# A decoder block on one core: the attention phase with its heads regrouped by transfers within SBUF, and a new plan of steps

## The reference

```python
kv = _ln(x, kvn_w, kvn_b) @ kv_w + kv_b              # k and v, 16 heads of 32
q = (_ln(x, qn_w, qn_b) @ q_w + q_b).reshape(b, c, HEAD, HD).transpose(0, 2, 1, 3)
q = _rotary(q, x, rh_w, rh_b)
k = _rotary(k, x, rh_w, rh_b)
qn = _ln(q, ln_w, ln_b)                               # layer norm of each head's 32 values
kn = _ln(k, ln_w, ln_b)
scores = jnp.einsum('bhqd,bhkd->bhqk', qn, kn) / np.sqrt(HD).astype(np.float32)
attn = jax.nn.softmax(scores, axis=-1)
a = jnp.einsum('bhqk,bhkd->bhqd', attn, v)
return a.transpose(0, 2, 1, 3).reshape(b, c, dims) @ out_w + out_b
```

## Time and profile before

| | us |
|---|---|
| median of 3 runs (lowest, highest) | 2368.12 (2367.32, 2368.73) |
| the profiled execution: its time | 2366.49 |
| the profiled execution: its span on the core | 2364.7 |
| mean granted TensorE clock | 0.926 of full speed |

### The profile page before, as it was taken

The page is one execution under the profiler, slowest core; times in us unless marked ns, Lnnn a source line. Parts: engine busy times, 40 slices in busy tenths (PEclk is TensorE's granted clock), DMA queues, the critical chain, the costliest instruction groups (busy, mean ns, idle before and its releaser), DMA issues. The chain is left out here.

```text
span 2364.7 us, 31908 instructions
## 1 busy us (share of the span) xinstructions
PE 1990.4 (84%) x10328; PEld 1432.6 (61%) x10328; DVE 1609.8 (68%) x3007; ACT 1061.1 (45%) x1820; POOL 1025.8 (43%) x879
## 2 busy tenths in 40 slices
PE   4579989899898989989984999999948887878872
PEld 4446656665665656656533888887837666666651
DVE  4467777777777777877744666767544777777765
ACT  1246546464563645646552222222215456555653
POOL 1568668587685876858610222222101212222121
PEclk9689999999999999999987999999969999999885
DMA  3000010100001010010104121111031121022111
GB/s 131 0 28 1 15 42 1 55 1 28 28 1 55 1 31 25 1 36 1 36 1 171 41 87 53 53 53 53 19 111 36 54 72 56 15 71 72 54 36 54
DMA packets 54718, 99.24 MB, mean 42 GB/s; under 512 B 5040, under 2 KB 8112, under 8 KB 54576
## 3 DMA queue, kind: packets, MB, share of 16 engines
q1 hardware_dynamic: 54576, 97.38, 12.0%
HBM read 63.82 MB, written 33.55 MB: 41 GB/s over the span
## 5 line engine op out<-in xcount | busy, mean ns | idle before, releaser
L438 DVE TENSOR_REDUCE a_neg_max<-a_max 128x1 f32<-128x512 f32 x512 | 341.5, 686 | 146.0 <-PE a_max L702 143.2
L594 ACT ACTIVATE a_probs<-a_exp 128x512 f32<-128x512 f32 x512 | 285.4, 596 | 288.8 <-PE a_exp L717 285.8
L1421 POOL TENSOR_TENSOR f_mixed<-f_tw,f_beta 128x512 f32<-128x512 f32 x64 | 96.1, 1521 | 343.2 <-DVE f_beta L1520 169.3
L294 POOL TENSOR_TENSOR a_rstd<-a_rstd,a_minus_half 128x16 f32<-128x16 f32 x64 | 186.3, 2911 | 121.8 <-DVE a_rstd L423 121.8
L702 PE MATMUL a_max<-a_stack 96*128 96x512 f32 x512 | 232.4, 457 | 6.7 <-DVE a_neg_max L438 6.4
L580 ACT ACTIVATE a_stack<-a_exp 96x512 fp32r<-96x512 f32 x256 | 138.4, 590 | 140.3 <-PE a_exp L689 139.6
L674 PE MATMUL a_t<-a_w_hi,a_zT_hi 128*128 128x384 f32 x512 | 176.5, 345 | 29.0 <-DVE a_v L406 29.0
L717 PE MATMUL a_exp<-a_stack 100*128 100x512 f32 x512 | 186.8, 407 | 5.4 <-ACT a_probs L594 3.4
L702 PEld LDWEIGHTS a_max<-a_stack 96*128 96x128 f32 x512 | 98.4, 193 | 145.9 <-issue 81.1
L971 POOL TENSOR_TENSOR r_part<-r_part 128x512 f32<-128x512 f32 x32 | 45.8, 1431 | 313.8 <-DVE r_part L1018 313.8
L689 PE MATMUL a_exp<-a_ident,a_n 128*96 128x128 f32 x1024 | 142.8, 283 | 43.3 <-ACT a_stack L580 35.1
(11 more groups left out here) (239 smaller groups left out, 5220.0 us busy)
## 6 DMA issues: line engine op xcount, KB each, us to landing
a_z<-x SPq DMA_DIRECT2D x8, 1024.0 KB, 5.6
a_y<-x SPq DMA_DIRECT2D x32, 256.0 KB, 2.7
x<-a_y SPq DMA_DIRECT2D x32, 256.0 KB, 2.2
r_xn<-x SPq DMA_DIRECT2D x8, 1024.0 KB, 5.6
r_cn<-ctx SPq DMA_DIRECT2D x8, 1024.0 KB, 7.7
x<-r_xn SPq DMA_DIRECT2D x8, 1024.0 KB, 4.3
f_xn<-x SPq DMA_DIRECT2D x8, 1024.0 KB, 5.5
x<-f_xn SPq DMA_DIRECT2D x8, 1024.0 KB, 7.2
```

The costliest lines, as they stand in the source:

```text
L294: nc.gpsimd.tensor_tensor(rstd[:, c], rstd[:, c], minus_half[:, :], ALU.pow).then_inc(pool_step, 1)
L438: nc.vector.tensor_reduce(neg_max[:, t, ROW + h:ROW + h + 1], bank_max[i % 2][:, :], AX_X, ALU.max, negate=True).then_inc(max_done, 1)
L594: nc.scalar.activation(probs[:, kt % 2, h, :], bank_exp[i % 2][:, :], ACT.Exp, scale=float(1.0 / np.sqrt(np.float32(HD)))).then_inc(exp_do ...
```

## The change

The normalised heads are no longer laid out as `n3`, transposed head by head and copied by ACT. Instead PE transposes the four heads of a group at once (`turn_heads`, 4 transposes for k and 4 for q), ACT and DVE split the result into `nT_hi` and `nT_lo` (`turn_high`, `turn_low`), and SP issues 24 DMAs per unit from SBUF to SBUF (`regroup`), each of 32 partitions x 512 values (64 KB), that put the pieces where `stack` wants them. The first score matmul of each head waits for that head's six DMAs (`stacked[h]`). Side 0 is now k (`SIDES`), which is only divided by its deviation; head weight and bias are folded in on the side of q. The x norm moves from DVE to ACT (`x_norm`), the bias of the output to POOL (`add_bias`), the x statistics from g = 0 to g = 2 and 3, the x transposes from the start of g = 1 into g = 0 (`z_item`), the four quarters of `normalise` to steps 15, 15, 0 and 1. The maxima are transposed and saved at step 14 of the unit before. All waits for PSUM banks that are shared among four uses (`bank_t`) are written out (`project_item`, `turn_item`, `out_item`, `z_item`). x comes and goes in whole batches.

```diff
-DVE_STEPS = 60
-
-
-
-
-NORM_AFTER, MEAN_AFTER, VAR_AFTER, LOW_AFTER = (-1, -1, -1, 1), (-1, 1), (3, 9), (14, 15)
-SAVE_AFTER, STATS_AFTER = (3, 4, 8, 10), (5, 8, 10, 14)
-PROJECT_STEPS = 10
-KEYS_FROM = 4
-WEIGH_AT = (8, 9, 11, 12, 14, 15)
-
-ATTN_LOW_AFTER = 6
-OUT_AT, ADD_AFTER = (12, 13, 15, 15), (11, 13, 14, 15)
-HIGH_AFTER = (2, 3)
+DVE_STEPS, POOL_STEPS = 55, 40
+
+
+QS_DONE = tuple(T * HG * min(i + 1, 14) // 14 for i in range(16))
+KS_DONE = tuple(T * HG * min(i, 12) // 12 for i in range(16))
+PROJECT_DONE = (3, 5, 6, 8, 10, 11, 13, 15, 16, 16, 16, 16, 16, 16, 16, 16)
+WEIGH_AT, SUM_AT = (5, 8, 11, 14), (6, 9, 12, 14)
+TURN_AT, SAVE_AFTER = (9, 11), (2, 4, 7, 9)
+OUT_AT, ADD_AFTER, OUT_BANK = (10, 12, 15, 15), (11, 13, 15, 15), (1, 1, 0, 1)
+Z_AT, Z_HIGH_AT, Z_LOW_AFTER = (13, 13, 14, 14), (13, 13, 15, 15), (13, 14, 15, 15)
+MAX_AT, SAVE_MAX_AT = 14, 14
+X_NORM_AT, STATS_AFTER, FINAL_AFTER, SHIFT_AFTER = (5, 6, 7, 8), (6, 8, 10, 12), 6, 12
+MEAN_AFTER, VAR_AFTER, SQUARE_AT = (0, 1), (3, 4), (1, 2)
+TURN_HIGH_AT, TURN_LOW_AFTER = (10, 12), (11, 13)
+NORM_AFTER, ATTN_HIGH_AT, ATTN_LOW_AFTER = (15, 15, 0, 1), 2, 3
+SIDES = (1, 0)
...
+            def regroup(U, par):
+
+                if counts(U - 1):
+                    sp.wait_ge(keyscore_done, T * HG * (U - 1))
+                sp.wait_ge(nTlo_done, 2 * U + 2)
+                for h in range(HG):
+                    src = slice(h * HD, (h + 1) * HD)
+                    for j, c, parts in ((h, 0, (nT_hi, nT_lo, nT_hi)), (HG + h, 1, (nT_hi, nT_hi, nT_lo))):
+                        for r, part in enumerate(parts):
+                            sp.dma_start(stack[r * HD:(r + 1) * HD, par, j, :].bitcast(F32), part[src, c, :].bitcast(F32)).then_inc(stacked[h], 16)
+
+            def unit(b, g, left, more):
+                if left >= 2:
+                    regroup(G * b + g + 2, g % 2)
+                if g == 0 and counts(b):
+                    sp.wait_ge(y_sum, T * (b + 1))
+                    sp.dma_start(rows(x1, b - 1), y[:, :, :]).then_inc(x1_out, 16)
+                if g == 1:
+                    if counts(b):
+                        sp.wait_ge(x1_out, 16 * b)
+                    sp.dma_start(y[:, :, :], rows(x, b)).then_inc(y_in, 16)
+                    if more:
+                        sp.wait_ge(zT_done, T * (b + 2))
+                        sp.dma_start(z[:, :, :], rows(x, b + 2)).then_inc(x_in, 16)
+
             sp.dma_start(z[:, :, :], rows(x, 0)).then_inc(x_in, 16)
             for dst, src in loads:
                 sp.dma_start(dst, src).then_inc(load, 16)
             for dst, src in loads_w:
                 sp.dma_start(dst, src).then_inc(load_w, 16)
-
...
+            def head_norm(U, s):
+
+                c = SIDES[s]
+                pool.wait_ge(var_done, 2 * U + s + 1)
                 nc.gpsimd.tensor_tensor(rstd[:, c], rstd[:, c], minus_half[:, :], ALU.pow).then_inc(pool_step, 1)
                 pool.wait_ge(pool_step, steps.next())
-                nc.gpsimd.tensor_tensor(n[:, c], n[:, c], wide(rstd[:, c]), ALU.mult).then_inc(pool_step, 1)
-                pool.wait_ge(pool_step, steps.next())
-                hw, hb = (a[:, :].unsqueeze(1).broadcast_to((P, T * HG, HD)) for a in (head_w, head_b))
-                nc.gpsimd.tensor_tensor(n[:, c], n[:, c], hw, ALU.mult).then_inc(pool_step, 1)
-                pool.wait_ge(pool_step, steps.next())
-                nc.gpsimd.tensor_tensor(n[:, c], n[:, c], hb, ALU.add).then_inc(n_done, 1)
-
...
-                new_x = g == 0 and left == 4
-                if g == 1 and left == 4:
-                    z_low(b + 1)
-                for i in range(-1, T * HG):
-                    if left >= 1 and i >= 0:
-                        row_max(U + 1, i)
+                for i in range(T * HG):
+                    if left >= 1:
+                        for m in within(QS_DONE, i):
+                            row_max(U + 1, m)
                     for c in range(T):
...
+            def turn_high(U, s, bank):
+                c = SIDES[s]
+                act.wait_ge(nT_done, 2 * U + s + 1)
+                if s == 0 and counts(U):
+                    for h in range(HG):
+                        act.wait_ge(stacked[h], 6 * 16 * U)
+                nc.scalar.activation(nT_hi[:, c, :], bank[:, :], ACT.Copy).then_inc(nThi_done, 1)
...
+                for i in range(T * HG):
+                    for m in within(KS_DONE, i):
+                        exps(U, m)
+                    if i == ATTN_HIGH_AT and counts(U):
+                        attn_hi(U - 1, (g - 1) % G)
+                    for s in range(2):
+                        if left >= 2 and i == SQUARE_AT[s]:
+                            square(U + 2, s)
+                        if left >= 2 and i == TURN_HIGH_AT[s]:
+                            turn_high(U + 2, s, bank_t[0 if g == 0 else s])
+                    for t in range(T):
+                        if g == 0 and left == 4 and i == X_NORM_AT[t]:
+                            x_norm(b + 1, t)
+                        if g == 0 and left == 4 and i == Z_HIGH_AT[t]:
+                            z_high(b + 1, t)
+                    if i == SAVE_MAX_AT and left >= 1:
+                        save_max(U + 1, (g + 1) % 2)
...
+            def turn_heads(U, s, bank):
+
+                c = SIDES[s]
+                pe.wait_ge(n_done, 2 * U + s + 1)
+                for t in range(T):
+                    last = nc.tensor.transpose(bank[:, t * P:(t + 1) * P],
+                                               n[:, c, t * HG:(t + 1) * HG, :].rearrange("p h i -> p (h i)"), ident[:, :])
+                last.then_inc(nT_done, 1)
...
-                    pe.wait_ge(stack_saved, 2 * (HG * U + h + 1))
+                    pe.wait_ge(stacked[h], 6 * 16 * (U + 1))
...
+            def turn_item(b, g, left, s):
+
+                U = G * b + g
+                if g == 0 and s == 1:
+                    pe.wait_ge(nTlo_done, 2 * (U + 2) + 1)
+                elif left >= 3:
+                    pe.wait_ge(qkv_saved, T * (U + 3) + 3 + s)
+                else:
+                    pe.wait_ge(y_sum, T * b + 3 + s)
+                turn_heads(U + 2, s, bank_t[0 if g == 0 else s])
+
...
+            def z_item(b, t):
+
+                U = G * b
+                if t == 0:
+                    pe.wait_ge(nTlo_done, 2 * (U + 2) + 2)
+                elif t >= 2:
+                    pe.wait_ge(zlo_done, T * (b + 1) + t - 1)
+                elif counts(b):
+                    pe.wait_ge(y_sum, T * b + 2)
+                else:
+                    pe.wait_ge(qkv_saved, T * (U + 3) + 4)
+                transpose_z(b + 1, t)
+
...
+            def unit(b, g, left, more):
+                U = G * b + g
+                for i in range(T * HG):
+                    if left >= 1:
+                        for m in within(QS_DONE, i):
+                            query_scores(U + 1, (g + 1) % 2, m)
+                    if left >= 3:
+                        for m in within(PROJECT_DONE, i):
+                            project_item(b, g, left, m)
+                    for m in within(KS_DONE, i):
+                        key_scores(U, g % 2, m)
+                    if i in WEIGH_AT:
+                        weigh(U, g, WEIGH_AT.index(i))
+                    if i in SUM_AT:
+                        sum_rows(SUM_AT.index(i))
+                    if i == MAX_AT and left >= 1:
+                        transpose_max(U + 1)
+                    for s in range(2):
+                        if left >= 2 and i == TURN_AT[s]:
+                            turn_item(b, g, left, s)
+                    for t in range(T):
+                        if g == 0 and left == 4 and i == Z_AT[t]:
+                            z_item(b, t)
```

More of the change, by code:

```diff
@@ L82, in end, with within @@
         self.base, self.n = self.start + passes * self.per, 0
+def within(done, i):
+    return range(done[i - 1] if i else 0, done[i])
 def attention_phase(nc, x, x1, w):
@@ L329, in _ @@
+            run(pool, unit, steps, POOL_STEPS)
         @block.vector
@@ L490, in unit @@
                     if left >= 3 and i in SAVE_AFTER:
                         save_qkv(U + 3, (g + 3) % G, SAVE_AFTER.index(i))
-                    if new_x and i in STATS_AFTER:
-                        x_stats(b + 1, STATS_AFTER.index(i))
+                    for s in range(2):
+                        if left >= 2 and i == TURN_LOW_AFTER[s]:
+                            turn_low(U + 2, s, bank_t[0 if g == 0 else s])
+                    if g == 2 and more and i in STATS_AFTER:
+                        x_stats(b + 2, STATS_AFTER.index(i))
@@ L494, in unit @@
+                    if g == 3 and more and i == FINAL_AFTER:
+                        x_final(b + 2)
+                    if g == 3 and more and i == SHIFT_AFTER:
+                        x_shift(b + 2)
+                    for t in range(2):
+                        if g == 0 and counts(b) and i == ADD_AFTER[t]:
```

(8 more changed lines are left out.)

513 lines of the change are left out of this document (238 added, 275 removed).

## The result

| | before | after |
|---|---|---|
| median (lowest, highest), us | 2368.4 (2367.3, 2368.7) | 2457.9 (2455.8, 2458.3) |
| span of the profiled execution | 2364.7 | 2456.2 |
| mean granted TensorE clock | 0.926 | 0.897 |

What follows compares the result with a forecast made beforehand. PE was taken to bound the kernel before, DVE's queue the unit heads after; 38 - 7 - 4 - 13 + 22 = +36 on 2366.5 gave 2402.5, as median 2404 us, range 2335 to 2450.

Steps and rivals of the forecast that it cites:

- The mechanism: Ordinary units: PE's work falls by 2.5 us, but PE waits 3.4 for transfers at 20 unit heads and loses clock.
- the price of the transfers: Unit heads: 0.45 us per 64 KB issue and 1.9 landing, 4.2 together, leaving PE idle 3.4.
- SP issues six DMAs: Unit heads: six issues on SP come before the next unit's first score matmul can start.
- issue is the bound: Rival, SP's transfers: 1.03 us per issue adds 3 to 4 at each of 20 heads, about +90, 2490; chance 0.10.
- The clock: Half clock behind waits: 0.8 us at each of 20 heads, 1 at each g = 0 end, +22, bounds 0 and 60.
- the sum: Whole kernel: 38 ordinary units, -7 g = 0 units, -4 last batch, -13 start, +22 clock, giving +36 us.
- The head as DVE's queue: Unit start to eighth score matmul: DVE's queue of 14.7 us sets the time, ordinary unit 30.8 instead of 30.4.
- The row sums at zero: Row sums "one step behind" on PE: stand alike in both orders, so priced at zero.
- the prices of the prediction: PE work: an isolated product or row sum 1.2 us, a product and sum directly behind one another 1.9.
- Start and last batch: Start up to the first `attn_hi`: -13 us, bounds 5 and 20 off; last batch: -4 of 115.3.
- Two small steps of the working: Unit heads: first score matmul 3.9 us after the last row sum; DVE's first maximum from 2.8 to 4.4, moving everything 1.7.
- The network is unchanged: Behind attention: retention and the network stay unchanged, a difference of 0.

Runs made afterwards that it cites:

- k_early: Changed kernel with SP issuing the key-side copies of heads 0 and 1 behind the first low half instead of the second: 2404.9 us.
- act_zs: Changed kernel with loads ahead of transfers, row sums directly behind products, key side of heads 0 and 1 issued earlier, ACT issuing head 0's query side: 2358.1 us.
- best1: act_zs with head 0's six copies ahead of all others, SP issuing the key side and one query-side copy, ACT the other two: 2335.6 us.
- best2: best1 with the high and low halves of the query side one step earlier: 2315.8 us.
- z_first: Changed kernel with the loads of y and the next x ahead of the 24 transfers on SP in units with g = 1: 2435.5 us.
- best2_behind: best2 with the row sums of key tiles 0 to 2 one step behind their products again: 2355.5 us.
- best3: best2 with the second variance of a unit after step 6 instead of step 4: 2325.1 us.
- before_sums: Kernel before the change with the row sums of key tiles 0 to 2 directly behind their products: 2402.5 us.
- before_two: Kernel before the change with only the row sums of key tiles 0 and 1 directly behind their products: 2389.3 us.

## Why the prediction was out of its range

- **The mechanism was right**: the transposes' work left PE, a wait for transfers came at the heads of g = 2, 3 and 0, and the half clock behind it. The head of g = 1 has no wait for a transfer.
- **The failed term was the price of the transfers.** "For 64 KB I take 0.45 and 1.9": measured 0.63 and 2.0, inside the bounds of 0.44 to 1.03 but 1.0 more per wait (5 x 0.18 + 0.1), about 20 over 21 waits. I had drawn it from loads of 256 KB; none of those rows had the shape of 32 partitions. k_early, act_zs and best1 show this wait as the largest cost: together with the sums' position and the loads, 142 us lie between the changed kernel and best2.
- **The step left out was SP's queue behind the transfers.** "SP issues six DMAs" counted the queue ahead of the first score matmul only. The 18 others and two loads stand behind, with x at the end: z_first, 22 us. The rival "issue is the bound" had named that 24 issues fill most of a unit; they filled 15 of 34, and what it missed was the load behind them.
- **The clock was sized about right.** 0.8 per head was taken; stretches with equal waits show 0.8 (k_early) and 0.5 (best1). The units took 36 more than the sum gave them (+89 for +53). The waits (20) and x (22) are 42, so the rest of the sum, the clock's 22 in it, was if anything some 6 too high. This is a remainder and no measurement.
- **The head as DVE's queue: near.** 30.8 was reckoned without waits. best2_behind, with the waits nearly gone (and the halves one step earlier), has 30.9, 31.4 and 30.2: 92.5 for three, against 92.4. Only the total is confirmed, not what DVE's queue is made of: taking 0.9 from it in best3 gained nothing.
- **The row sums at zero: right for the change**, since both orders place them alike. Three pairs for six isolated ones come to 1.5 by the prices of the prediction; they are worth 1.1 in an ordinary unit (best2_behind against best2, 22.8 in 21) and only where a sum covers no wait.
- **Start and last batch**: -8.3 for -13 and -0.2 for -4, together 8.5 more than forecast. With the 36 of the units and 10.8 behind attention these are the 55.5 between +36 and +91.5.
- **Two small steps of the working don't add up.** From 4.2 less 0.5 the first score matmul would start 3.7 behind the last row sum, not 3.9, and from 2.8 to 4.4 DVE's first maximum moves by 1.6, not 1.7. It is some 2 to 6 us in the whole and changes no reading.
- **"The network is unchanged": its code is, its time isn't.** Of the +10.8 behind attention 2.7 stand between the last `attn_hi` and retention's first matmul, 0.8 in retention, 7.3 in the network. There one DVE instruction starts late with nothing that the profile shows to wait for, once in each of the changed kernel and its eleven versions (7.0 to 7.6), and not in the kernel before, before_sums or before_two:

```profile
2096.57 0.69 DVE L1553 TENSOR_REDUCE f_sums<-f_w 128x4 f32<-128x512 f32 x1 [7.35 <-issue]
```

The network took 635 to 639 in all versions of the changed kernel and 630 to 631 in the three of the kernel before. The instruction queues moved 0.9 MB in the changed kernel and 1.9 before, so the code is fetched differently; that this is the cause was not tested and stays open.

## What to carry over

Price a copy by its issue as well as its landing, list everything that stands in the issuing queue behind it, loads for other stages too, and issue first what the next consumer needs, from two engines if the issues are longer than the landing. A product or sum "one step behind" is worth its place where it stands between a producer and a consumer on another engine and costs where it doesn't: the same edit gave -33 and +34 us. Filling a wait with other work helps only if no other queue ends the stretch. And price a short wait or a lower clock between two points that the wait itself doesn't move.
